# A decoder layer on one core: a head's values transposed by VectorE in 32x32 blocks instead of by TensorE

## The reference

```
q = x @ Wq
latent_kv = (x @ Wk + x @ Wv) @ W_down_kv
k_rec, v_rec = latent_kv @ W_up_k, latent_kv @ W_up_v
# 16 heads of 16 channels each, per batch: 32 heads in all
scores = (qh @ kh.T) * scale * exp(-1e-4 * |i - j|)      # 1024 x 1024 for a head
out = softmax(scores) @ vh                               # 1024 x 16 for a head
return out @ Wo
```

## Time and profile before

| | |
|---|---|
| three runs | 620.94, 621.41, 622.21 us |
| profiled execution, first to last instruction (span; the page gives no other time for it) | 622.1 us |
| PE busy | 555.1 us, 89% |
| ACT busy | 398.9 us, 64% |
| DVE busy | 372.7 us, 60% |
| POOL busy | 213.1 us, 34% |
| attention loop, 32 heads | from 60 to 323 us |
| TensorE's granted clock, mean of the span | 0.967 |

### The profile page before, as it was taken

One profiled execution on the slowest core, in us unless ns is written; L12 is line 12 of the kernel. 1 busy time (PEld: TensorE's weight loads), 2 busy tenths in 40 slices (PEclk: granted clock), 3 DMA queues, 4 the chain that ended last, 5 costly groups with the idle time before them and its releaser, 6 DMA issues.

```text
span 622.1 us, 14225 instructions
## 1 busy us (share of the span) xinstructions
PE 555.1 (89%) x4551; PEld 299.5 (48%) x4552; DVE 372.7 (60%) x999; ACT 398.9 (64%) x570; POOL 213.1 (34%) x238
## 2 busy tenths in 40 slices
PE   3996999999999999999999899999988789999910
PEld 2442333333333333333346677776654566666600
DVE  5796565555556555555545588878857634444436
ACT  4477899999999999999982556554333533333311
POOL 4000692494059400000003433443275524444420
PEclk9997899999999999999999999999988999999975
DMA  9923343344444333443406610000022234443257
GB/s 255 369 79 66 68 76 66 73 79 78 77 79 80 73 72 72 76 73 73 95 2 183 193 33 2 3 1 2 32 95 77 100 112 128 127 135 130 98 178 262
DMA packets 53547, 60.20 MB, mean 97 GB/s; under 512 B 10721, under 2 KB 44642, under 8 KB 53506
## 3 DMA queue, kind: packets, MB, share of 16 engines
q1 hardware_dynamic: 47570, 47.24, 31.6%
q0 software_dynamic: 3792, 10.36, 4.7%
q10 hardware_dynamic: 2144, 2.10, 1.0%
HBM read 22.17 MB, written 18.61 MB: 66 GB/s over the span
## 4 chain that ended last, share of the span: by engine, by line
PE 73%; DVE 9%; DMA 6%; issue 4%; ACT 4%; POOL 1%; another core or an unknown queue 1%; DVEq 1%; SPq 1%; ACTq 0%; POOLq 0%
PE ps L712 20%; PE ps L702 20%; PE ps L1098 8%; PE ps L1115 4%; DMA x_slots<-val,place_i 3%; PE ps L754 2%; PE ps L855 2%; PE ps L923 2%; PE ps L721 2%; DMA val<-y_tok 2%; PE ps L1090 2%; DVE ftmp L1762 2%; PE ps L630 1%; PE ps L873 1%; PE ps L891 1%
## 5 line engine op out<-in xcount | busy, mean ns | idle before, releaser
L1618 DVE TENSOR_TENSOR ps<-ps,kstack 128x128 f32<-128x128 f32 (+3 forms) x256 | 123.8, 495 | 105.9 <-PE ps L702 105.9
L1246 ACT ACTIVATE pT<-ps 128x1024 f32<-128x1024 f32 x128 | 124.6, 1023 | 6.3 <-PE ps L702 2.7
L702 PE MATMUL ps<-qstack,kstack 96*128 96x512 bf16 x352 | 93.6, 389 | 4.5 <-issue 4.5
L712 PE MATMUL ps<-pT,vcur 128*32 128x256 f32 x1024 | 80.5, 387 | 0.0
L1246 ACT ACTIVATE xn<-ps 128x1024 f32<-128x1024 f32 x64 | 65.5, 1024 | 10.2 <-PE ps L702 9.2
L1246 ACT ACTIVATE xnT<-ps 128x1024 f32<-128x1024 f32 x64 | 65.2, 1019 | 0.2
L583 POOL DMA_INDIRECT y_tok<-ftmp,dest_i x47 | 45.0, 958 | 58.5 <-DVE ftmp L2030 57.9
L1098 PE MATMUL ps<-parts,xnT 128*128 x188 | 52.6, 403 | 6.3 <-issue 5.6
L702 PEld LDWEIGHTS ps<-qstack,kstack 96*128 96x128 bf16 x352 | 29.2, 98 | 54.9 <-issue 15.2
L1423 ACT ACTIVATE oT<-ps 128x128 f32<-128x128 f32 x47 | 13.0, 277 | 61.8 <-PE ps L1098 54.1
L556 POOL TENSOR_TENSOR resid<-resid,projb 128x512 f32<-128x512 f32 x8 | 10.1, 1265 | 122.0 <-DVE xn L1955 121.4
(11 more groups left out here) (301 smaller groups left out, 962.4 us busy)
## 6 DMA issues: line engine op xcount, KB each, us to landing
qstack<-parts SPq DMA_DIRECT2D x132, 64.0 KB, 2.3
x_slots<-wcur SPq DMA_DIRECT2D x1, 6016.0 KB, 20.5
kT<-x_slots SPq DMA_DIRECT2D x47, 128.0 KB
kstack<-parts SPq DMA_DIRECT2D x132, 32.0 KB, 2.0
early<-parts SPq DMA_DIRECT2D x60, 64.0 KB, 2.3
resid<-in_x_dram SPq DMA_DIRECT2D x4, 512.0 KB, 6.9
parts<-in_L_ffn_Wg_dram SPq DMA_DIRECT2D x16, 128.0 KB, 2.3
parts<-in_L_ffn_Wu_dram SPq DMA_DIRECT2D x16, 128.0 KB, 2.2
```

Source lines behind the costliest of these rows:

```text
L702: nc.tensor.matmul(ps[:, score_bank(g3, kt) + g, :], kstack[g3][:, kt * P:(kt + 1) * P], qstack[g3][:, 1 - first, 512 * g:512 * (g + 1)], ...
L712: mm = nc.tensor.matmul(ps[2 * HD * g:2 * HD * (g + 1), 6 + r, 0:256], vcur[:, r, kt, :], pT_ring[kt % 4][:, 256 * g:256 * (g + 1)], start ...
L1246: nc.scalar.activation(pT_ring[kt % 4], two_banks(score_bank(g3, kt)).rearrange("p a n -> p (a n)"), ACT.Exp, bias=-SHIFT).then_inc(s_exp, 1)
L1618: nc.vector.tensor_tensor(blk, blk, within[:, side, 4 * P - n:] if side == 0 else within[:, side, 0:n], ALU.mult)\
```

## The change

The transposition moves to VectorE. A transposition on VectorE turns each 32 x 32 block within itself and leaves the blocks where they are, so the queries must be dealt out differently first. Before, column group g took queries 256g to 256g+255 of each step, contiguous in the buffer. Now it takes queries 32g to 32g+31 out of every 128: eight runs of 32 f32 columns, 128 columns apart. The output columns stay 256 in a row. With that, block t of partitions 32g to 32g+31, turned within itself, is what partitions 32g to 32g+31 need for query tile t, and one VectorE transposition of 128 x 256 out of PSUM replaces the copy. The two transpositions of TensorE go (two per head), with the semaphores `s_ot` and `s_on`; `normalise` reads SBUF in place of PSUM and waits for VectorE's own transposition. TensorE's values of the head after next wait for `s_ob` (the bank was read out) and no longer for `s_on` (it was normalised).

```
--- before.py
+++ after.py
@@ weighted (TensorE)
                 if kt == 0:
                     pe.wait_ge(s_vcur, n + 1)
-                    after(pe, s_on, n - 1)
+                    after(pe, s_ob, n - 1)
                 for g in range(4):
-                    mm = nc.tensor.matmul(ps[2 * HD * g:2 * HD * (g + 1), 6 + r, 0:256], vcur[:, r, kt, :],
-                                          pT_ring[kt % 4][:, 256 * g:256 * (g + 1)], start=(kt == 0), stop=(kt == ST - 1),
-                                          tile_position=(0, 2 * HD * g))
+                    out_g = ps[2 * HD * g:2 * HD * (g + 1), 6 + r, 0:256].rearrange("p (t q) -> p t q", q=2 * HD)
+                    mm = nc.tensor.matmul(out_g, vcur[:, r, kt, :],
+                                          pT_ring[kt % 4].rearrange("p (t g q) -> p g t q", g=4, q=2 * HD)[:, g, :, :],
+                                          start=(kt == 0), stop=(kt == ST - 1), tile_position=(0, 2 * HD * g))
                 mm.then_inc(s_pv, 1)
-
-            def out_transposes(n, r):
-
-                pe.wait_ge(s_ob, n + 1)
-                for c in range(2):
-                    mm = nc.tensor.transpose(ps[:, 6 + r, 256 + c * P:256 + (c + 1) * P], obT[:, c * P:(c + 1) * P], ident[:])
-                mm.then_inc(s_ot, 1)
@@ head_steps (TensorE), and after the loop
-                    if kt == 4 and not first:
-                        out_transposes(n - 1, 1 - r)
...
                 out_begin()
-                out_transposes(n, 1)
                 out_first()
@@ read_out, normalise (VectorE)
             def read_out(n, r):
                 dve.wait_ge(s_pv, ST * (n + 1))
-                after(dve, s_ot, n)
-                nc.vector.tensor_copy(obT[:], ps[:, 6 + r, 0:256]).then_inc(s_ob, 1)
-
-            def normalise(n, r):
-
-                dve.wait_ge(s_ot, n + 1)
-                o = ps[:, 6 + r, 256:512].rearrange("p (c g d) -> p g c d", c=2, g=4)
-                nc.vector.reciprocal(rinv8[:].rearrange("p (g c) -> p g c", c=2), o[:, :, :, HD])
-                nc.vector.drain()
-                nc.vector.tensor_tensor(att[:, ds(n // H * ST, ST), ds(n % H * HD, HD)].rearrange("p (g c) d -> p g c d", c=2),
-                                        o[:, :, :, 0:HD],
-                                        rinv8[:].rearrange("p (g c) -> p g c", c=2).unsqueeze(3).to_broadcast([P, 4, 2, HD]),
-                                        ALU.mult).then_inc(s_on, 1)
+                nc.vector.transpose(obT[:], ps[:, 6 + r, 0:256]).then_inc(s_ob, 1)
+
+            def normalise(n):
+
+                dve.wait_ge(s_ob, n + 1)
+                o = obT[:].rearrange("p (t d) -> p t d", d=2 * HD)
+                nc.vector.reciprocal(rinv8[:], o[:, :, HD])
+                nc.vector.drain()
+                nc.vector.tensor_tensor(att[:, ds(n // H * ST, ST), ds(n % H * HD, HD)], o[:, :, 0:HD],
+                                        rinv8[:].unsqueeze(2).to_broadcast([P, ST, HD]), ALU.mult)
```

More of the change, by code:

```diff
@@ L297, in decoder_layer @@
         s_fs = sem("s_fs"); s_diag = sem("s_diag"); s_exp = sem("s_exp"); s_pv = sem("s_pv"); s_vcur = sem("s_vcur")
-        s_ob = sem("s_ob"); s_ot = sem("s_ot"); s_on = sem("s_on"); s_att = sem("s_att")
+        s_ob = sem("s_ob"); s_att = sem("s_att")
         s_cT_ps = sem("s_cT_ps"); s_cT = sem("s_cT"); s_ck_ps = sem("s_ck_ps"); s_ck = sem("s_ck")
@@ L1649, in head_steps @@
                     if kt == ST - 2 and not first:
-                        normalise(n - 1, 1 - r)
+                        normalise(n - 1)
             dve.wait_ge(s_pool, 8)
@@ L1660, in _ @@
                 read_out(B * H - 1, 1)
-                normalise(B * H - 1, 1)
+                normalise(B * H - 1)
             def finish(b, half, j, n, qt):
```

## The result

The changed kernel took 617.05 us in the median of 7 runs (614.43 to 620.51), the kernel before, run beside it, 621.55 us (7 runs). The ratio is 0.9924, with a 95% interval of 0.9899 to 0.995. Two repeats with 12 runs each gave 616.04 against 621.47 us, ratio 0.9937 (0.9902 to 0.9971), and 622.08 against 623.92 us, ratio 0.9942 (0.9911 to 0.9974). A ratio is estimated from all fast runs and is not the quotient of the two medians; those quotients scatter more, from 0.9913 to 0.9971.

What follows compares the result with a forecast made beforehand. The prediction took TensorE, by its own instructions, to bound the kernel. 7.9 us from the removed transpositions less 0.2 us for late stacks made 7.7 us, taking the median from 621.4 to 613.7 us, range 612.5 to 617.5.

Steps and rivals of the forecast that it cites:

- likeliest case: Whole kernel: the forecast itself comes about, 612.7 to 614.8 us, chance 0.74.
- strided reads at half their price: Values matmuls: reads cost half the break-even of 16 ns per record, gain 4 us, 617.5 us; smaller gain 0.04.
- The transpositions of TensorE: Attention loop: removing two per head gains 0.26 us, 7.8 us for heads 1 to 30.
- The 0.13 us of head 31: Last head: ScalarE follows closely, so removing TensorE's transpositions gains only 0.13 us there.
- The dealt-out queries: Values matmuls: reading the moving operand in eight runs of 32 columns costs 0; upper end 25 us in all.
- The rival with strided reads: Values matmuls: strided reads cost TensorE time, at worst 638 us; chance 0.11, of which 0.07 no gain or loss.
- The transposition on VectorE: Each head: takes 0.45 to 0.5 us in place of the copy; up to about 0.9 us nothing is lost.
- The multiplication was 292 ns and should be no slower: Normalisation on VectorE: reading SBUF, it stays covered ahead of the decay of kt = 7, cost 0.
- This is lost once: 0.2 us: Near head 8: faster TensorE asks too early for the stack SyncE loads; lost once, not per head.
- well under 10.6 us: Attention loop: sign expected in the profile after, SyncE's waits for the scores (L702) fall from 10.6 us.
- Slow VectorE transposition: Each head: at 1.67 us the transposition makes the kernel 636 us, break-even 1.16 us; chance 0.05, nearly all slower.
- ScalarE as the bound: Attention loop: ScalarE loses its 0.5 us reserve per head, time stays at 620 to 621.5 us; chance 0.04.

Runs made afterwards that it cites:

- stride_only: The kernel before with only the queries dealt out in runs of 32 columns, TensorE still transposing: ratio 1.0003, loop 244.44 us against 244.64.
- psum_norm: The changed kernel with VectorE's transposition written to PSUM, where the normalisation reads it: 620.31 us against 622.51 for the kernel before, ratio 0.9953, loop 237.84 us.
- vcur_act: The changed kernel with transposed outputs kept in PSUM and the copy of a head's values moved to ScalarE: ratio 0.9908 to the kernel before, loop 237.38 us.
- few_both: The changed kernel with ten stack loads per head from the fourth, transposed outputs in PSUM and the values' copy on ScalarE: loop 236.43 us.
- no_pool: The changed kernel without GpSimd's splits of later units' queries and keys, one fill with zeros instead: loop 236.51 us.

## Why the prediction was right in its direction and 3 us too low

That the time lies inside the range is luck in part. The likeliest case was 612.7 to 614.8, and the upper end of 617.5 stood for strided reads at half their price, which did not come about; what filled this room were losses that the sum didn't hold.

- **The transpositions of TensorE, 7.8 us in the loop: right.** With both disturbances gone the loop takes 236.43 us, 8.2 less than before; the sum said 7.8 from pairs that were free of disturbance, and 244.64 - 30 x 8.14 = 0.4 us of disturbance stood in the loop before. That two records of 273 ns give back 0.26 us, not 0.55, was read rightly from the chain. The 0.13 us of head 31 came as 0.14 (11.05 us from its first scores to the first matmul of the projection, now 10.91).
- **The dealt-out queries, 0: right,** by stride_only and by 1.00 us per values step. The rival with strided reads falls.
- **The transposition on VectorE, 0.45 to 0.5 us and free to about 0.9: right.** It takes 0.44 us; the room is 0.84 us. The estimate beside the Trainium skill's 311 ns (VectorE: DVE Perf Modes, The three transpose paths) was 0.44 us.
- **"The multiplication was 292 ns and should be no slower": wrong, and worth some 0.6 us of the profiled loop (heads 8 and 9).** It looked at the median and at how many elements pass, and not at where the operands lie. Before, the multiplication read PSUM and was 294 ns at most, also in the eleven heads in which it started inside a GpSimd instruction; now both inputs are in SBUF, and when it starts inside one it ends some 0.15 us behind it. The copy was held up in the kernel before as well (1230 ns at most), and that one the prediction did not look at either. The Trainium skill has this as a rule, SBUF — State Buffer, section Who interferes with whom: VectorE and GpSimd share a pair of ports, taken as an exclusive lock, and "A DVE instruction with two SBUF inputs contends with a GpSimd instruction that reads SBUF". By that rule a copy from SBUF to SBUF in a two-port mode is held too, the transposition out of PSUM is not, and the reciprocal with its one input is not. The trace agrees in all four: 1175, 1177, 450 and, for the reciprocal, 205 ns at most. It was the rule to weigh against this change.
- **"This is lost once: 0.2 us" (the stacks): the right mechanism, and a size that varies.** In the profiled execution after the change TensorE never waited for keys. In the repeats it did twice (0.35 and 0.31 us) and once (0.27), in psum_norm and vcur_act once each (0.54 and 0.52). The lead had been read from one execution, and the long issues of SyncE, already seen in that trace, fall elsewhere in each. SyncE's waits in the loop, forecast "well under 10.6 us", are 8.4 us, as their row shows:
```profile
SPq L407 <- PE ps L702: 8.4, 16, 0.7
```
Both disturbances together, measured against few_both's loop, cost 0.9 to 1.8 us in the three traces of the changed kernel; the sum had 0.2.
- **What the sum left out: everything behind the loop. This is the larger part.** It carried a gain of 7.7 us through 300 us of straight code unchanged. The loops are 6.4 to 7.3 us shorter, the three ratios mean 3.6 to 4.7 us. So in each comparison 2 to 4 us are not kept, and 0.3 to 1.8 us even where the interval's end that favours the change is taken. One part is seen in every execution and has no known cause: 1.4 us in the loop over the tiles. The half clock at the first tiles (2.2 and 1.2 us) and VectorE's unnamed waits come and go. No execution had both, and whether the change makes either likelier can't be told from this many executions: the one followed a wait of over 5 us in five of eleven executions with the changed loop and in none of three with the old one, the other was there in six of eleven and in all three.
- **Rivals.** Slow VectorE transposition and ScalarE as the bound didn't come about. No variant beat the changed kernel by more than the measurement tells: vcur_act's interval overlaps its own three.

## What to carry to other kernels

When an operand moves from PSUM to SBUF, or a step with only SBUF operands is added, look first at what GpSimd does at that time, and read the maximum of a line, not its median. A queue that needs 7.6 of every 7.88 us has no lead to spare: read its longest issues, from the whole trace, before a faster engine is set upon it. And a gain in one loop is to be followed through the stages behind it, in more than one execution: compare stage by stage, at which clock each runs, and tell apart what every execution repeats from what comes and goes.

## What the runs showed of the hardware

- A 32x32-block transposition of 128x256 f32 took 440 ns from PSUM to SBUF (rows above), and 453 to 465 ns from PSUM to PSUM.
- A VectorE copy from SBUF to SBUF waited for a GpSimd fill to end: 9.51 us instead of 0.22 (no_pool). A multiplication of two SBUF operands ended some 0.15 us behind the GpSimd instruction in which it started, up to 1175 ns instead of 293; out of PSUM it took 294 ns at most beside the same instructions.
- A TensorE transposition of 128 f32 columns behind others cost 0.11 us of the chain.
- Single load issues of SyncE took 0.9 to 1.9 us instead of 0.59, about every 12 us up to some 125 us into the span, in every kernel and without GpSimd's splits too; why is open.
